# A graph kernel's softmax stage: the sixth running sum of every ten moves from VectorE to TensorE

## The reference

```
w_m = (efeat @ W_msg + b_msg).reshape(E, in_f, -1)
w_a = (efeat @ W_attn + b_attn).reshape(E, in_f, -1)
h_src = feat[src][:, :, None]
e1 = w_m * h_src
e2 = w_a * h_src
seg_max = jax.ops.segment_max(e2, dst, num_segments=N)
ex = jnp.exp(e2 - seg_max[dst])
denom = jax.ops.segment_sum(ex, dst, num_segments=N)
attn = ex / denom[dst]
ft = jax.ops.segment_sum(e1 * attn, dst, num_segments=N)
return ft.sum(axis=1)
```

## Time and profile before

| | |
|---|---|
| median of three timed runs | 9802.14 us |
| profiled execution | 9803.99 us |
| span of the profiled execution | 9802.2 us |
| softmax stage, first to last carry multiplication (line 1721) | 3097.2 to 6498.6 us |
| whole span: PE, DVE, ACT, POOL busy | 7922.8, 7334.4, 3069.3, 7346.5 us |
| granted TensorE clock, whole span | 0.934 |

### The profile page before, as it was taken

One profiled execution on the slowest core, in us unless ns is written; L12 is line 12 of the kernel. 1 busy time (PEld: TensorE's weight loads), 2 busy tenths in 40 slices (PEclk: granted clock), 3 DMA queues, 4 the chain that ended last, 5 costly groups with the idle time before them and its releaser, 6 DMA issues.

```text
span 9802.2 us, 134013 instructions
## 1 busy us (share of the span) xinstructions
PE 7922.8 (81%) x37203; PEld 4272.0 (44%) x37203; DVE 7334.4 (75%) x13651; ACT 3069.3 (31%) x12664; POOL 7346.5 (75%) x5210
## 2 busy tenths in 40 slices
PE   0899995999993777777777777755999995899994
PEld 0565553555551333333333333323665554555552
DVE  2566562444545999999999999987887885788884
ACT  0111111000004777777777777742000000000000
POOL 5788886777767777777777777745888887688887
PEclk6999996999996999999999999977999997899997
DMA  1333332222223777777776777766222221333332
GB/s 31 100 107 100 98 97 51 58 68 63 64 55 74 205 203 201 200 201 205 203 202 200 201 204 203 202 178 193 79 82 69 82 69 46 100 106 99 99 103 49
DMA packets 491778, 1213.47 MB, mean 124 GB/s; under 512 B 237032, under 2 KB 274360, under 8 KB 470892
## 3 DMA queue, kind: packets, MB, share of 16 engines
q1 hardware_dynamic: 242522, 994.11, 31.7%
q0 software_dynamic: 213680, 110.92, 9.1%
q10 hardware_dynamic: 35440, 106.85, 3.3%
HBM read 417.99 MB, written 787.23 MB: 123 GB/s over the span
## 4 chain that ended last, share of the span: by engine, by line
POOL 37%; issue 26%; DVE 20%; PE 14%; DMA 2%; DVEq 1%; SPq 1%; ACT 0%; POOLq 0%; ACTq 0%
POOL arena L559 36%; PE PS L949 12%; DVE arena L1687 5%; DVE arena L1691 4%; DVE arena L1733 3%; DVE arena L1700 2%; PE PS L971 2%; DVE arena L1711 2%; DVE arena L1813 1%; DVEq L1679 1%; DVE arena L1422 0%; DVE tmp L1815 0%; DVE arena L1721 0%; DVE arena L1814 0%; DMA arena<-d_lane 0%
## 5 line engine op out<-in xcount | busy, mean ns | idle before, releaser
L949 PE MATMUL PS<-arena,TB 125*128 125x500 bf16 (+1 forms) x18711 | 4048.0, 372 | 137.7 <-DVE arena L1390 92.6
L559 POOL DMA_INDIRECT arena<-d_feat,srci x1650 | 2580.0, 1564 | 842.0 <-issue 454.4
L949 PEld LDWEIGHTS PS<-arena,TB 125*128 125x128 bf16 x18711 | 1836.5, 100 | 2023.3 <-issue 198.1
L559 POOL DMA_INDIRECT arena<-d_h,srci x1518 | 1975.8, 1302 | 612.6 <-issue 452.6
L770 ACT ACTIVATE arena<-PS,arena 125x32 f32<-125x32 f32 x10560 | 2020.3, 446 | 303.2 <-PE PS L1068 262.8
L1390 DVE TENSOR_SCALAR arena<-arena,lane 125x2000 bf16<-125x2000 f16 (+3 forms) x1848 | 1208.5, 713 | 368.4 <-PE PS L949 243.8
L559 POOL DMA_INDIRECT arena<-d_rel,irel x858 | 1206.6, 1406 | 306.3 <-issue 261.4
L1402 DVE SCALAR_TENSOR_TENSOR arena<-arena,lane,PS 128x500 f32<-128x500 f16 x891 | 631.7, 711 | 1002.5 <-PE PS L949 847.0
L559 POOL DMA_INDIRECT arena<-d_nn,srci x759 | 1071.9, 1412 | 282.2 <-issue 230.6
L1115 PE MATMUL PS<-arena,ident 125*125 125x512 f32 x1650 | 873.8, 610 | 407.5 <-ACT arena L813 212.1
L1733 DVE SCALAR_TENSOR_TENSOR arena<-arena 125x512 f32<-125x512 f32 x1155 | 863.0, 747 | 20.3
(11 more groups left out here) (274 smaller groups left out, 7174.9 us busy)
## 6 DMA issues: line engine op xcount, KB each, us to landing
d_soft_max<-arena SPq DMA_DIRECT2D x165, 1120.0 KB
d_soft_den<-arena SPq DMA_DIRECT2D x330, 560.0 KB
d_soft_num<-arena SPq DMA_DIRECT2D x330, 560.0 KB
d_x<-arena ACTq DMA_DIRECT2D x165, 241.7 KB
arena<-d_x SPq DMA_DIRECT2D x165, 241.7 KB
d_rel<-arena SPq DMA_DIRECT2D x50, 669.4 KB
arena<-d_pick SPq DMA_DIRECT2D x33, 875.0 KB
arena<-d_lane SPq DMA_DIRECT2D x33, 875.0 KB
```

Source lines behind the costliest of these rows:

```text
L559: gp.indirect_dma_start(out=dst, out_offset=None, in_=table, in_offset=bass.IndirectOffsetOnAxis(ap=index, axis=0)).then_inc(S(sem), 16)
L949: ins = pe.matmul(PS[:, acc_at(L, q):acc_at(L, q) + w], TB[:, part, g * LANES * F:(g + 1) * LANES * F], OH[L][i][:, g, at:at + w], start=g ...
```

## The change

Sum 5 of each block, which VectorE made, is made by TensorE. Two new functions do it: `mid_rest` (row 5 times the identity) and `mid_sum` (sum 4 times a diagonal of the keeps of column 5), which add up in bank 2. VectorE's sum 6 reads its predecessor from that bank and waits for the semaphore `soft_mid`. ScalarE copies bank 2 into XS (`mid_rows`), and it builds a second diagonal in `last_keep`. Bank 2 also holds the products of group 1, so these are moved: instead of before step n = 0 they come before step n = 4, after a wait until `mid_rows` is done (`soft_mrow`). `mid_rest` stands in step n = 1 and `mid_sum` in step n = 2, each behind the waits of that step. VectorE's sums are now written out one by one, with `weigh` 4 ahead of sum 3. Three semaphores of the work after the stage are merged into others, at the same places. The new lines of after are not the lines of the profile; the names are the same.

```diff
+MID = B1 // 2
+SUMS = B1 - 3
...
-        DG = ar(o, P); o += P
+        DG = ar(o, 2 * P).rearrange("p (n c) -> p n c", n=2); o += 2 * P
...
             def last_keep(b, s):
 
-                act.activation(DG, ident[0:P, 0:P], ACT.Copy, scale=KR[:, s, B1 - 1, 1:2])
+                for n, t in enumerate((MID, B1 - 1)):
+                    act.activation(DG[:, n, :], ident[0:P, 0:P], ACT.Copy, scale=KR[:, s, t, 1:2])
+
+            def mid_rows(b, s):
+
+                act.wait_ge(S("soft_mid"), b + 1)
+                act.wait_ge(S("soft_sum"), SUMS * b + MID)
+                act.activation(XS[:, s, 1:3, MID, :], PS[0:P, 1024:1536].rearrange("p (a c) -> p a c", a=2),
+                               ACT.Copy).then_inc(S("soft_mrow"), 1)
...
                            .then_inc(S("soft_exp"), 1)
+                        if n == 2 and (not first or s >= 1):
+                            mid_rows(b - 1, (s + 2) % 3)
                     else:
...
+            def mid_rest(b, s):
+
+                pe.wait_ge(S("soft_prod"), NG3 * (b + 1) + (2 if not isinstance(b, int) or b < NB1 - 1 else 0))
+                pe.wait_ge(S("soft_num"), 5 * b + MID // 2 + 1)
+                bank = PS[0:P, 1024:1536].rearrange("p (a c) -> p a c", a=2)
+                pe.matmul(bank, ident[0:P, 0:P], XS[:, s, 1:3, MID, :], start=True, stop=False)
+
+            def mid_sum(b, s):
+
+                pe.wait_ge(S("soft_sum"), SUMS * b + MID - 1)
+                bank = PS[0:P, 1024:1536].rearrange("p (a c) -> p a c", a=2)
+                pe.matmul(bank, DG[:, 0, :], XS[:, s, 1:3, MID - 1, :], start=False, stop=True).then_inc(S("soft_mid"), 1)
...
                 bank = PS[0:P, 3072:3584].rearrange("p (a c) -> p a c", a=2)
-                pe.matmul(bank, DG, XS[:, s, 1:3, B1 - 2, :], start=True, stop=False)
+                pe.matmul(bank, DG[:, 1, :], XS[:, s, 1:3, B1 - 2, :], start=True, stop=False)
...
                     products(b + 1, ahead, k1, 0)
-                    products(b + 1, ahead, k1, 1)
 
                 for n in range(6):
+                    if n == 4 and left >= 1:
+                        if not first or s >= 1:
+                            pe.wait_ge(S("soft_mrow"), b)
+                        products(b + 1, ahead, k1, 1)
                     if n == 4 and left >= 2:
...
                     if n == 1 and (not first or s >= 1):
                         pe.wait_ge(S("soft_row"), b)
+                        mid_rest(b - 1, (s + 2) % 3)
+                    if n == 2 and (not first or s >= 1):
+                        mid_sum(b - 1, (s + 2) % 3)
                     bank = PS[0:P, (6 + n % 2) * 512:(7 + n % 2) * 512]
...
             first_sum(NB1 - 1, 2)
             pe.wait_ge(S("soft_done"), NB1 - 1)
+            mid_rest(NB1 - 1, 2)
+            mid_sum(NB1 - 1, 2)
             pe.wait_ge(S("soft_carry"), NB1)
             last_sum(NB1 - 1, 2)
...
-                for t in range(1, B1 - 1):
+                def add(t):
+
                     to, last = XS[:, s, 1:3, t, :], XS[:, s, 1:3, t - 1, :]
                     if t == 1:
                         dve.wait_ge(S("soft_first"), b + 1)
                         last = PS[0:P, 3584:4096].rearrange("p (a c) -> p a c", a=2)
+                    elif t == MID + 1:
+                        dve.wait_ge(S("soft_mid"), b + 1)
+                        last = PS[0:P, 1024:1536].rearrange("p (a c) -> p a c", a=2)
                     else:
-                        if t % 2 == 0:
-                            dve.wait_ge(S("soft_num"), 5 * b + t // 2 + 1)
-                        dve.wait_ge(S("soft_sum"), (B1 - 2) * b + t - 1)
-                    ins = v.scalar_tensor_tensor(to, last, KR[:, s, t, 1:2], to, ALU.mult, ALU.add)
-                    ins.then_inc(S("soft_sum"), 1)
-                    yield
-                    if t % 2:
-                        weigh(t + 1)
-                        yield
+                        dve.wait_ge(S("soft_sum"), SUMS * b + (t - 1 if t < MID else t - 2))
+                    if t % 2 == 0:
+                        dve.wait_ge(S("soft_num"), 5 * b + t // 2 + 1)
+                    v.scalar_tensor_tensor(to, last, KR[:, s, t, 1:2], to, ALU.mult, ALU.add).then_inc(S("soft_sum"), 1)
+
+                add(1)
+                yield
+                weigh(2)
+                yield
+                add(2)
+                yield
+                weigh(4)
+                yield
+                add(3)
+                yield
+                add(4)
+                yield
+                weigh(6)
+                yield
+                yield
+                add(6)
+                yield
+                add(7)
+                yield
+                weigh(8)
+                yield
+                add(8)
+                yield
```

More of the change, by code:

```diff
@@ L490, in store @@
             def store(b, s, done):
-                sp.wait_ge(S("soft_sum"), (B1 - 2) * b + B1 // 2 - 1)
+                sp.wait_ge(S("soft_sum"), SUMS * b + MID - 1)
                 put(b, s, 0, 0, B1)
@@ L776, in first_rows @@
                 act.wait_ge(S("soft_first"), b + 1)
-                act.wait_ge(S("soft_sum"), (B1 - 2) * b + 1)
+                act.wait_ge(S("soft_sum"), SUMS * b + 1)
                 act.activation(XS[:, s, 1:3, 0, :], PS[0:P, 3584:4096].rearrange("p (a c) -> p a c", a=2),
@@ L832, in _ @@
             first_rows(NB1 - 1, 2)
+            mid_rows(NB1 - 1, 2)
             last_rows(NB1 - 1, 2)
@@ L835, in _ @@
             act.activation(FT[:, :, :], FT[:, :, :], ACT.Exp).then_inc(S("ce"), 1)
-            act.wait_ge(S("hd"), 1)
-            act.activation(HM[:, 0:2, :], HM[:, 0:2, :], ACT.Exp).then_inc(S("he"), 1)
+            act.wait_ge(S("cd"), 3)
+            act.activation(HM[:, 0:2, :], HM[:, 0:2, :], ACT.Exp).then_inc(S("ce"), 1)
             for n in range(NCH):
@@ L1078, in first_sum @@
                 pe.matmul(bank, ident[0:P, 0:P], SC, start=False, stop=True).then_inc(S("soft_first"), 1)
+            def mid_rest(b, s):
[7 more added lines that the diff above has]
+                pe.matmul(bank, DG[:, 0, :], XS[:, s, 1:3, MID - 1, :], start=False, stop=True).then_inc(S("soft_mid"), 1)
             def last_sum(b, s):
-                pe.wait_ge(S("soft_sum"), (B1 - 2) * (b + 1))
+                pe.wait_ge(S("soft_sum"), SUMS * (b + 1))
                 bank = PS[0:P, 3072:3584].rearrange("p (a c) -> p a c", a=2)
-                pe.matmul(bank, DG, XS[:, s, 1:3, B1 - 2, :], start=True, stop=False)
+                pe.matmul(bank, DG[:, 1, :], XS[:, s, 1:3, B1 - 2, :], start=True, stop=False)
                 pe.matmul(bank, ident[0:P, 0:P], XS[:, s, 1:3, B1 - 1, :], start=False, stop=True)\
@@ L1151, in _ @@
                 ins = pe.transpose(PS[0:P, 1024 + a * 128:1024 + (a + 1) * 128], YT[:, a, 0:P], ident[:, :])
-            ins.then_inc(S("cbk"), 1)
+            ins.then_inc(S("ct"), 1)
             pe.wait_ge(S("l_w6"), 16 * 15)
@@ L1787, in _ @@
                     v.tensor_tensor_scan(YT[:, n + a, 1:P + 1], FT[:, a, :], CT[:, n + a, :], 0.0, ALU.mult, ALU.add).then_inc(S("cc"), 1)
-            dve.wait_ge(S("cbk"), 1)
+            dve.wait_ge(S("ct"), 2)
             link(v.tensor_copy(CB, PS[0:P, 1024:1024 + ROW]))
@@ L1793, in _ @@
             v.tensor_tensor(HM[:, 0, :], HG[:, 0:CH], HM[:, 2, :], ALU.subtract)
-            v.tensor_tensor(HM[:, 1, :], CB[:, 0:CH], HM[:, 2, :], ALU.subtract).then_inc(S("hd"), 1)
-            dve.wait_ge(S("he"), 1)
+            v.tensor_tensor(HM[:, 1, :], CB[:, 0:CH], HM[:, 2, :], ALU.subtract).then_inc(S("cd"), 1)
+            dve.wait_ge(S("ce"), 2)
             for part, m in ((HG, 0), (CB, 1)):
```

## The result

The changed kernel takes 10087.68 us (median of 4 runs, 10062.77 to 10122.78), the kernel before 9803.74 (median of 4). The ratio is 1.0294, with a 95% interval of 1.0281 to 1.0308. I had forecast slower, but by 191 us and in a range that ends at 10,055; it is slower by 284.

The account below looks back on a forecast made before the run. VectorE, busy 2460.40 of 2500 us, was taken to set the pace. 162 blocks at +1.18 us each (period 21.94 against 20.76) add 191 us to 9803.99, giving 9993 for a timed run (72%); range 9905 to 10,055.

Parts of the forecast that it names:

- The step that failed: On TensorE, a sign of being right: the granted clock stays at 1.00, since its gaps get smaller.
- at no cost: On TensorE, `mid_rest`, 0.86 us, goes into the gap before step 2, where 1.30 us are idle.
- The main term: VectorE waits 1.5 us ahead of sum 6 for `mid_sum`, queued behind step 2's wait; period 21.94, +1.18 us per block.
- The saving on VectorE: Without sum 5, VectorE alone would have a period of 20.30, 0.46 us less per block.
- TensorE and ScalarE alone: A loop without VectorE, with 1.0 us of slack, takes 1.69 us more: +0.69 per block, 9914 us; chance 10%.
- slower yet: TensorE idles ahead of group 1 products that wait for `mid_rows`: 81 us more, 10,074; chance 9%.
- Faster: VectorE alone sets the pace, sum 6 being ready in time: -0.46 us per block, 9727 us; chance 6%.

Follow-up runs that it names:

- e7: Kernel before, all sums on VectorE, with the group 1 products moved ahead of step 4 and a second diagonal that nobody reads; 9865.91 us, ratio 1.0056.
- e1: Changed kernel with four more bf16 matmuls per block on TensorE between step 0 and step 1, their output overwritten by `mid_rest`; 10008.66 us, ratio 1.0207.
- e2: Changed kernel with `mid_rest` moved ahead of step 1's waits; 10007.87 us, ratio 1.0206.
- e10: Kernel of e6 with `mid_sum` put back behind step 2's wait for step 0's exponential; 9944.27 us, ratio 1.0140.
- e6: Kernel of e5 with `scalable` moved ahead of the group 1 products; 9773.42 us, ratio 0.9966.
- e9: Kernel of e6 with the other diagonal, that of column 9, also built at the head of ScalarE's block; 9716.84 us, ratio 0.9912.
- e8: Kernel before with only the group 1 products moved ahead of step 4; 9819.07 us, ratio 1.0011.
- e4: Changed kernel with `mid_rest` ahead of step 1's waits and `mid_sum` ahead of step 2's waits; 9851.41 us, ratio 1.0047.
- e5: Kernel of e4 with the diagonal of column 5 built at the head of ScalarE's block instead of in its long stretch; 9816.93 us, ratio 1.0010.

## Why the prediction was wrong

**The step that failed** is the sentence "The granted clock stays at 1.00, the 2.4 GHz level, since TensorE's gaps get smaller". The gaps got smaller in sum (4.5 us of idle time per block before, 3.7 after, by the stage's two lines), and one of them got longer. This is the gap ahead of step 1 in the kernel before:

```profile
5032.89 1.02 PE L1115 MATMUL PS<-arena,ident 125*125 125x512 f32 x2
...
5035.96 1.09 PE L1115 MATMUL PS<-arena,ident 125*125 125x512 f32 x2 [1.19 <-DVE arena L1691]
```

It was 1.19 us and became 1.83 to 1.93, 1.87 on average. Three things made it longer. In the ordinary block shown above, whose first product is at 5026.88, they are:

- Step 0 starts earlier, since the group 1 products don't stand ahead of it any more (t = 10.59 instead of 10.85), and its last pair starts 0.19 earlier (t = 11.52 instead of 11.71).
- The copy of sum 0 that ends the gap starts 0.27 later (t = 13.20 instead of 12.93), by the diagonal and by the late scaled column. (The row of before names a maximum of VectorE as the releaser, but the one that step 1 needs is the thirteenth, and it had ended; the copy ends at 34.97 + 0.85 = 35.82, just before.)
- TensorE goes on later after that copy. Before, step 1 starts 35.96 - 35.82 = 0.14 after its end, and e7 has 0.15. Here `mid_rest` starts 41.26 - 40.92 = 0.34 after it. It stands behind two waits of its own (`soft_prod` and `soft_num`) that were met long before, and in the trace TensorE's sequencer passes them between 5041.01 and 5041.20.

The parts add up to 0.19 + 0.27 + 0.20 = 0.66 us, and 1.83 - 1.19 is 0.64. The first two follow from my own working; the third is in it nowhere, since `mid_rest` was to go into idle time "at no cost". e7 has the first two alone, with a gap of 1.57 to 1.70 us and no fall of the clock. No run takes away the two waits alone.

After the longer gap the clock falls in 71 of 162 blocks, at 23.15 - 21.98 = 1.17 us each: 83 us. e1 and e2 take this away in two ways and win 79 and 80 (81 and 82 if each kernel is measured against the kernel before that ran beside it). The scatter fits it: the four runs of the changed kernel lie within 60 us of one another, the slowest at a mean clock of 0.919 and the fastest at 0.927; those of e1 and e2, without falls of the clock in the stage, within 3.2.

**The main term was right and somewhat small.** The period of an undisturbed block was to be 21.94 and is 21.98. Before, it was 20.75 (without the last, as here; I had used 20.76), which makes 1.23 x 162 = 199 us instead of 191. The last distance, 18.13 instead of 17.11, adds 1. 199 + 1 + 83 = 283, and 284 were measured. Piece by piece, from the block that begins at 5026.88, with ScalarE's line of the long stretch, the two diagonals, the copy of sum 0 and the exponentials of steps 0 and 1:

```profile
5033.59 2.95 ACT L772 ACTIVATE arena<-PS,arena 125x32 f32<-125x32 f32 x16 [1.62 <-PE PS L1081]
...
5036.79 0.81 ACT L786 ACTIVATE arena<-ident,arena 125x125 f32<-125x125 f32 x2
...
5040.08 0.84 ACT L780 ACTIVATE arena<-PS 125x512 f32<-125x512 f32 x1
...
5043.27 1.47 ACT L823 ACTIVATE arena<-PS 125x512 f32<-125x512 f32 x2
```

| | worked out | this block | mean of the ordinary blocks |
|---|---|---|---|
| long stretch begins | 6.82 | 6.71 | 6.80 |
| step 0's exponential begins | 16.53 | 16.39 | 16.48 |
| `mid_sum` begins | 17.59 | 17.50 | 17.60 |
| sum 6 begins | 18.74 | 18.75 | 18.84 |
| from sum 6 to the next block | 3.20 | 3.11 | 3.15 |

That the place of `mid_sum` in the queue causes it is shown by e10 against e6: 171 us for this one edit, 1.09 x 163 = 178 by the periods.

**The saving on VectorE** was to be 0.46 per block. e9 shows it once nothing stands in its way: 20.73 - 20.17 = 0.56. More than the 0.10 on top comes from two pairs of dependent instructions that are shorter than in my rows: in e9 the two maxima ahead of sum 6 take 0.91 where I had 1.00, and `weigh` 8 takes 0.72 to sum 8 where it took 0.80 before. I did not test why.

**The rival "TensorE and ScalarE alone"** had the right outline and the wrong slack. I took the idle time ahead of the group 2 products, 1.0 us, for the slack of the loop. But the loop doesn't go through that gap alone: it goes through ScalarE's scaled column and step 4's exponential, where the slack was 0.36 (e7, e8, and the table under e4). Its price of 9914 was wrong in the other direction too, since it charged `mid_sum` with 0.96, which e4 hides in the gap ahead of step 2; e4 has this loop at 9851.

**The rival "slower yet"** with late group 1 products did not come: from 3500 to 6000 us none of the matmuls of the group 1 products waits for `mid_rows`; only their weight loads do, while step 3 still runs. **"Faster"** needed an early `mid_sum`; in e9, where it does not wait for the exponential, VectorE's wait is gone.

**What stays open.** What makes the clock fall in one block and not in the next isn't settled. It isn't the length of the gap ahead of `mid_rest`: from 3500 to 6000 us it is 1.87 us on average and 1.83 to 1.93 at the ends of its range, in the slow blocks and in the ordinary ones alike. A gap of at most 1.70 in e7 brings no fall; nothing between 1.70 and 1.83 was run.

## What to carry to other kernels

When one engine is 98% busy, look for the loops of the others that are just as long: an instruction taken from the busy engine is worth nothing until the partner that takes it over stands ahead of the waits that it doesn't need (171 us here), and its helpers stand in idle time instead of in the other engines' loop (57 us for one diagonal, e6 to e9, and 34 for the other, e4 to e5). The slack of such a loop is read link by link along the loop, not from the longest idle time on one of its engines. And check each gap of TensorE by itself: less idle time in sum with one longer gap can cost the clock. An instruction that is put into such a gap behind the wait that ends it brings its own waits along, and they lengthen the gap.

## What the runs showed of the hardware that I had not expected

TensorE's clock can fall to the lower level in a loop where TensorE is busy 84% of the time and no gap is longer than 1.93 us (from 3500 to 6000 us), and in this kernel all 71 falls come 0.1 to 1.4 us after the work has begun again, none in the gap. Where two more waits, long met, stood ahead of TensorE's next matmul, it began 0.34 us after the end of the copy that it waited for; without them it took 0.14 (before) and 0.15 (e7). Four useless matmuls per block in that gap made the kernel 79 us faster (e1). A ScalarE exponential right behind other ScalarE work lasts 0.71 to 1.00 us from start to end against 0.60 after a pause, and an engine that waits for its end waits for that difference too.
